# GNN kernel: first stage only counts, sum matrices built later and kept in SBUF, second bias split between PE and VectorE

## The reference, cut to what matters

```python
deg  = segment_sum(ones, dst) + 1 ;  dinv = rsqrt(deg)
conv(x, W, b) = segment_sum((x@W)[src] * dinv[src]*dinv[dst], dst) + dinv**2 * (x@W) + b
x  = l2norm(conv(x0, W1, b1))
f(z) = conv(l2norm(conv(z, Wf1, bf1)), Wf2, bf2) + z
k1 = f(x); k2 = f(x + 0.5*k1); k3 = f(x + 0.5*k2); k4 = f(x + k3)
x  = conv(x + (k1 + 2*k2 + 2*k3 + k4)/6, W2, b2)
```

## Time and profile before

| | |
|---|---|
| median of 3 runs | 9125.33 us (9120.25 to 9130.2) |
| the profiled execution, its time | 9196.13 us |
| span of the profile | 9194.4 us |
| busy: PE, DVE, POOL, ACT | 6718.1, 6441.7, 5499.4, 3381.1 us |
| DMA moved | 1693.27 MB, 184 GB/s over the span |
| first two blocks of `prepare` | until 482.5 us |
| scatter of x | until about 1012 us |
| `local_pass` | about 1042 to 3256 us |
| coupled stages | 3256.9 to about 7560 us |
| attention | to the end |

### The profile page before, as it was taken

The page is one execution under the profiler, slowest core; times in us unless marked ns, Lnnn a source line. Parts: engine busy times, 40 slices in busy tenths (PEclk is TensorE's granted clock), DMA queues, the critical chain, the costliest instruction groups (busy, mean ns, idle before and its releaser), DMA issues. The chain is left out here.

```text
span 9194.4 us, 168134 instructions
## 1 busy us (share of the span) xinstructions
PE 6718.1 (73%) x36044; PEld 5385.6 (59%) x36044; DVE 6441.7 (70%) x17476; ACT 3381.1 (37%) x9316; POOL 5499.4 (60%) x6135
## 2 busy tenths in 40 slices
PE   1600399889988966988897797789666669996665
PEld 0100388888888844766675576667444545554544
DVE  2910388677877888779778977987798981117976
ACT  0000366666666645641361164136100111113323
POOL 0067687777877756755575476557332655545667
PEclk9655799999999977999999999999888985557889
DMA  9333345765444455879879988988898762214544
GB/s 142 86 97 97 100 145 146 123 141 139 143 144 138 139 147 156 249 241 292 250 244 312 315 253 260 335 271 259 280 308 280 210 174 61 60 56 141 169 142 125
DMA packets 1968800, 1693.27 MB, mean 184 GB/s; under 512 B 183280, under 2 KB 1879809, under 8 KB 1968301
## 3 DMA queue, kind: packets, MB, share of 16 engines
q1 hardware_dynamic: 1541549, 1107.88, 42.2%
q0 software_dynamic: 160192, 335.62, 13.1%
q10 hardware_dynamic: 266560, 244.12, 7.8%
HBM read 1063.01 MB, written 624.28 MB: 184 GB/s over the span
## 5 line engine op out<-in xcount | busy, mean ns | idle before, releaser
L1193 PE MATMUL bank<-c_rows,c_sums 128*128 128x256 f32 (+1 forms) x3920 | 1336.0, 425 | 1032.3 <-DVE c_rows L1284 620.7
L680 PE MATMUL bank<-wf_w,c_xt 128*128 128x256 f32 x6272 | 1539.2, 390 | 3.7 <-DVE y L1358 2.6
L1193 PEld LDWEIGHTS bank<-c_rows,c_sums 128*128 128x128 f32 x3920 | 696.7, 203 | 1396.9 <-DVE c_rows L1284 699.3
L1225 ACT ACTIVATE c_xt<-bank 128x512 f32<-128x512 f32 (+1 forms) x980 | 563.5, 575 | 2424.2 <-PE bank L1203 1408.8
L1166 POOL DMA_INDIRECT c_rows<-t_tab,src_row x784 | 872.5, 1113 | 970.7 <-PE bank L1193 807.4
L680 PEld LDWEIGHTS bank<-wf_w,c_xt 128*128 128x128 f32 x6272 | 1231.7, 197 | 185.5 <-issue 3.6
L1284 DVE SCALAR_TENSOR_TENSOR c_rows<-bank,carry,c_rows 32x256 f32<-32x256 f32 (+1 forms) x1950 | 910.6, 467 | 495.6 <-issue 340.5
L1166 POOL DMA_INDIRECT c_rows<-z_tab,src_row x784 | 768.9, 981 | 304.7 <-issue 193.0
L985 DVE TENSOR_TENSOR lx_lo<-bank,lx_hi 128x512 fp32r<-128x512 f32 (+1 forms) x1000 | 658.1, 658 | 350.8 <-ACT lx_hi L930 284.5
L930 ACT ACTIVATE lx_hi<-bank 128x512 fp32r<-128x512 f32 (+1 forms) x1000 | 561.1, 567 | 577.4 <-PE bank L899 457.0
L564 POOL DMA_INDIRECT x_tab<-x_in,stage_pos x396 | 406.3, 1026 | 599.5 <-DMA x_in<-in_x 479.3
(11 more groups left out here) (295 smaller groups left out, 15231.3 us busy)
## 6 DMA issues: line engine op xcount, KB each, us to landing
c_z<-z_tab SPq DMA_DIRECT2D x882, 256.0 KB
c_sums<-sum_tab SPq DMA_DIRECT2D x980, 128.0 KB
z_tab<-lz SPq DMA_DIRECT2D x400, 256.0 KB
t_tab<-lt SPq DMA_DIRECT2D x400, 256.0 KB
z_tab<-y ACTq DMA_DIRECT2D x392, 256.0 KB
c_own<-z_tab SPq DMA_DIRECT2D x392, 256.0 KB
t_tab<-y ACTq DMA_DIRECT2D x392, 256.0 KB
c_own<-t_tab SPq DMA_DIRECT2D x392, 256.0 KB
```

The costliest lines, as they stand in the source:

```text
L680: last = nc.tensor.matmul(out, x(k), w[:, k, :], start=(k == 0), stop=(k == ks - 1))
L1193: nc.tensor.matmul(psum[s % 2][:, i * win:(i + 1) * win], sums[:, s, i, :], rows[:, s, i, 0:win], start=True, stop=True).then_inc(S["summe ...
L1225: nc.scalar.activation(xt[:, s % 2].rearrange("p k n -> p (k n)")[:, 0:n], psum[2 + s % 2][:, 0:n], ACT.Copy).then_inc(S["copied"], 1)
```

## The change

- `prepare`, first block: `floats`, `rows` and `store` are gone from it. `hot_hi` comes from ACT: a Square of (column - upper bits) into a new buffer `away`, then a Relu of (1 - that) into `hot_hi`, 4 and 4 instructions of 396 columns per turn. DVE makes `hot_lo` only; PE waits for both.
- `prepare`, third block: `rows`, `floats` and `store` run here, in the first 49 of the 99 turns, with rings of 4.
- The sum matrices go to one SBUF tensor `sums_all` (100,352 bytes per partition), loaded in the first coupled stage and read by PE in all later ones; the loads of `c_sums` in the other nine stages and of `w_sums` are gone. SBUF for it comes from tensors that now end with `local_pass`.
- PE's part of a coupled stage is unrolled (no loop).
- End stages: the bias of one tile of the pair (r = 1, 2) or of both (r = 3) is a further matmul with 3 contraction rows in `multiply` (`c_degs` times `bf2_rows`); for r = 0 both stay on DVE. `c_degs` is made once (in the mid stage r = 0), stored to `deg_tab`, and loaded per pair by `load_others`.
- For r = 0 and 3 the first instruction of `add_rest` (1327, 1331) moves to ACT as `begin_rest`.
- Four scaled copies of bf2 are no longer made; in `shares_beside_far` several semaphores are merged.

```diff
-def skewed(eng, count, steps, ring=4):
+def skewed(eng, count, steps, ring=4, unrolled=False):
...
-    if turns < 1:
+    if unrolled or turns < 1:
...
+        prepare(nc, a, S, counts, m)
+        local_pass(nc, a, S, counts, m)
+    with nc.sbuf_tensor("sums_all", [P, TE, P], F32) as sums_all:
+        m["sums_all"] = sums_all
+        coupled_stages(nc, a, S, counts, m)
+        attention(nc, a, S, counts, m)
...
-                skewed(sp, turns, [(0, rows), (1, store)], ring=2)
...
+            @block.scalar
+            def _(act):
+                act.wait_ge(S["masks"], 7)
+                act.wait_ge(S["dst_split"], 1)
+
+                def high(j, s):
+                    if not isinstance(j, int) or j >= 1:
+                        act.wait_ge(S["hot_high"], ph.at("hot_high", j - 1))
+                    for i in range(4):
+                        last = nc.scalar.activation(away[:, i, :], cols[:], ACT.Square,
+                                                    bias=minus_hi[:, bass.ds(j * 4 + i, 1)])
+                    last.then_inc(S["away"], 1)
+                    act.wait_ge(S["away"], ph.at("away", j))
+                    for i in range(4):
+                        if not isinstance(j, int) or j >= 1:
+                            act.wait_ge(S["counted"], ph.at("counted", j - 1, i + 1))
+                        nc.scalar.activation(hot_hi[:, i, :], away[:, i, :], ACT.Relu, scale=-1.0, bias=ones[:, 0:1]
+                                             ).then_inc(S["hot_high"], 1)
+                skewed(act, turns, [(0, high), (1, lambda j, s: None)], ring=2)
...
-                        v.tensor_scalar(hot_hi[:, i, :], cols[:], dst_hi[:, t], None, ALU.is_equal)
...
-                skewed(dve, turns, [(0, floats), (0, hots)], ring=2)
+                skewed(dve, turns, [(0, hots), (1, lambda j, s: None)], ring=2)
...
+                        pe.wait_ge(S["hot_high"], ph.at("hot_high", j, i + 1))
...
+                def rows(j, s):
+                    if isinstance(j, int) and j >= builds:
+                        return
+                    if not isinstance(j, int) or j >= 4:
+                        sp.wait_ge(S["row_floats"], pb.at("row_floats", j - 4))
+                    sp.dma_start(rows_i[:, s, :], a["dst_rows"][bass.ds(j * (4 * P), 4 * P)].partition_broadcast(P)
+                                 ).then_inc(S["sums_in%d" % s], 16)
+
+                def store(j, s):
+                    sp.wait_ge(S["sums_built"], pb.at("sums_built", j))
+                    sp.dma_start(m["sum_tab"][bass.ds(j * 4, 4), :, :].rearrange("t p f -> p t f"),
+                                 sums[:, s, :, :]).then_inc(S["stored%d" % s], 16)
+                skewed(sp, builds, [(0, load), (0, rows), (3, store)])
+                for j in range(builds, turns):
+                    load(j, j % 4)
+                for s in range(4):
+                    sp.wait_ge(S["stored%d" % s], pb.ring_end("stored", s))
...
+                def floats(j, s):
+                    dve.wait_ge(S["sums_in%d" % s], pb.ring_at("sums_in", j, s))
+                    if not isinstance(j, int) or j >= 4:
+                        dve.wait_ge(S["stored%d" % s], pb.ring_at("stored", j, s, back=1))
+                    v.tensor_copy(rows_f[:, s, :], rows_i[:, s, :]).then_inc(S["row_floats"], 1)
+                    dve.wait_ge(S["row_floats"], pb.at("row_floats", j))
+                    for i in range(4):
+                        last = v.scalar_tensor_tensor(sums[:, s, i, :], rows_f[:, s, i * P:(i + 1) * P],
+                                                      dst_f[:, bass.ds(j * 4 + i, 1)], (up, down)[i % 2][:],
+                                                      ALU.is_equal, ALU.mult)
+                    last.then_inc(S["sums_built"], 1)
+                skewed(dve, builds, [(0, fill), (2, floats)])
+                for j in range(builds, turns):
+                    fill(j, j % 4)
...
+    if bias:
+        last = nc.tensor.matmul(out, bias[0], bias[1], start=False, stop=True)
...
+    by_pe = [(), (0,), (0,), (0, 1)][r] if end else ()
+    by_dve = [i for i in range(2) if i not in by_pe] if end else []
...
-    n_rest = [1, 1, 1, 4][r] + 1 if end else 1 if final else 0
+    n_rest = [1, 2, 2, 3][r] if end else 1 if final else 0
...
-                    sp.wait_ge(S["summed"], ph.at("summed", j - 4))
-                sp.dma_start(sums[:, s, :, :], m["sum_tab"][bass.ds(j * 2, 2), :, :].rearrange("t p f -> p t f")
-                             ).then_inc(S[f"sums_in{s}"], 16)
-                if past(j, 4):
                     sp.wait_ge(S["u_set"], ph.at("u_set", j - 4))
                 if first:
+                    sp.dma_start(sums[:, bass.ds(j * 2, 2), :],
+                                 m["sum_tab"][bass.ds(j * 2, 2), :, :].rearrange("t p f -> p t f")
+                                 ).then_inc(S[f"sums_in{s}"], 16)
...
+                if by_pe:
+                    sp.dma_start(degs[:, s, :].bitcast(F32), m["deg_tab"][:, bass.ds(j * (2 * P), 2 * P)]
+                                 ).then_inc(S[f"degs_in{s}"], 16)
...
+            if turned_degs:
+                sp.wait_ge(S["degs_split"], 2)
+                for n, part in enumerate((deg_hi, deg_hi, deg_lo)):
+                    for k, tiles_ in enumerate((P, TE - P)):
+                        sp.dma_start(m["deg_tab"][n].rearrange("(t p) -> t p", p=P)[k * P:k * P + tiles_, :],
+                                     part[0:tiles_, k, :].bitcast(F32)).then_inc(S["degs_out"], 16)
+                sp.wait_ge(S["degs_out"], 96)
...
-                    nc.tensor.matmul(psum[s % 2][:, i * win:(i + 1) * win], sums[:, s, i, :], rows[:, s, i, 0:win],
-                                     start=True, stop=True).then_inc(S["summed"], 1)
+                    nc.tensor.matmul(psum[s % 2][:, i * win:(i + 1) * win],
+                                     sums[:, j * 2 + i, :],
+                                     rows[:, s, i, 0:win], start=True, stop=True).then_inc(S["summed"], 1)
...
+                                        (degs[:, s, i * P:(i + 1) * P], m["bf2_rows"][0:3, :]) if i in by_pe else None)
...
-            skewed(pe, pairs, [(0, add_up(0)), (2, turn), (0, add_up(1)), (3, multiply)])
+            if turned_degs:
+                for k, tiles_ in enumerate((P, TE - P)):
+                    last = nc.tensor.transpose(psum[6][0:tiles_, k * P:(k + 1) * P],
+                                               m["c_root_deg"][:, k * P:k * P + tiles_], ident[:])
+                last.then_inc(S["degs_turned"], 1)
+            skewed(pe, pairs, [(0, add_up(0)), (2, turn), (0, add_up(1)), (3, multiply)], unrolled=True)
...
+            def begin_rest(j, s):
+                act.wait_ge(S[f"others_in{s}"], ph.ring_at("others_in", j, s))
+                if past(j, 2):
+                    act.wait_ge(S["taken"], ph.at("taken", j - 2))
+                nc.scalar.activation(rest[:, s % 2, :, :], zs[len(others) - 1][:, s, :, :], ACT.Copy,
+                                     scale=1.5 if r == 0 else -1 / 3).then_inc(S["rest_begun"], 1)
+
             def store(j, s):
                 act.wait_ge(S[done], ph.at(done, j))
                 act.dma_start(tiles(target, j, wout), y[:, s, :, 0:wout]).then_inc(S[f"stored{s}"], 16)
...
             if normed:
                 steps.append((ready, scale))
             steps.append((ready, store))
+            if begun:
+                steps.append((3, begin_rest))
...
-                    rest_step(v.tensor_scalar(pr, zs[0][:, s, :, :], 1.5, None, ALU.mult))
+                    pass
...
-                    rest_step(v.tensor_scalar(pr, zs[3][:, s, :, :], -1 / 3, None, ALU.mult))
+                    dve.wait_ge(S["rest_begun"], ph.at("rest_begun", j))
                     for n, c in enumerate((1 / 3, 2 / 3, 0.5)):
+                        if n:
+                            dve.wait_ge(S["rest_set"], ph.at("rest_set", j, count[0]))
+                        rest_step(v.scalar_tensor_tensor(pr, zs[n][:, s, :, :], c, pr, ALU.mult, ALU.add))
+                if by_dve:
+                    if r == 0:
+                        dve.wait_ge(S["rest_begun"], ph.at("rest_begun", j))
+                    else:
                         dve.wait_ge(S["rest_set"], ph.at("rest_set", j, count[0]))
-                        rest_step(v.scalar_tensor_tensor(pr, zs[n][:, s, :, :], c, pr, ALU.mult, ALU.add))
-                if end:
-                    dve.wait_ge(S["rest_set"], ph.at("rest_set", j, count[0]))
-                    for i in range(2):
-                        last = v.scalar_tensor_tensor(pr[:, i, :], m[f"bf2_{r}"][:], dinv[:, bass.ds(j * 2 + i, 1)],
+                    for i in by_dve:
+                        last = v.scalar_tensor_tensor(pr[:, i, :], scaled_bias[:], dinv[:, bass.ds(j * 2 + i, 1)],
                                                       pr[:, i, :], ALU.mult, ALU.add)
-                    last.then_inc(S["rest_set"], 1)
```

(3 more changed lines are left out.)

203 lines of the change are left out of this document (102 added, 101 removed).

## The result

| | before | changed | ratio |
|---|---|---|---|
| median of 4 runs | 9127.76 us (9120.25 to 9134.89) | 8850.49 us (8848.25 to 8863.71) | 0.9699, 95% interval 0.9683 to 0.9716 |
| profiled execution's span | 9194.4 us | 8850.1 us | |

The change saves 277 us; 263 were forecast.

The account below looks back on a forecast made before the run. Limits were taken stage by stage: DVE, then ACT, in the first block, POOL in the third and mid, DVE in end stages. -221 + 10 - 70 + 54 - 35 - 1 = -263 us from 9125.33 gave 8862 us, range 8790 to 8940.

Parts of the forecast that it names:

- First block, -221: First block: ACT becomes the limit at 4.55 us a turn, so the second block starts at 232 us instead of 453.
- rival B: First block: bound by hand-overs at 5.5 us a turn, not ACT's rate; +46, total 8908 us; chance 15%.
- Third block, +10: Third block: POOL stays the limit; the added casts, comparisons and DMA hide behind it but slow it by 10 us.
- rival C: Third block: POOL loses every DVE instruction in full, 88 us in place of 10; total 8940 us; chance 5%.
- the bound of 0 to 17: Third block: busy DVE and DMA slow POOL's 196 scatters by 17 us at most, 0 at least.
- sign of 530 to 545 us: Third block: the length expected in the changed kernel's profile if the prediction holds, 530 to 545 us.
- End r = 0, +54: End r = 0: DVE waits for begin_rest behind ACT's store, 1.50 us in place of 0.95; pair 4.05 to 4.60 us.
- Rival A: End r = 0 and 3: ACT runs ahead, begin_rest is in time; -49 and -70, total 8724 us; chance 10%.
- End r = 1 and 2, -70: End r = 1 and 2: DVE loses one bias addition worth 0.40 us; pair 4.32 to 3.96 us; bounds -78 and 0.
- Rival E: End r = 1 and 2: DMA holds the pair at 4.3 us, no gain; first block as forecast; total 8932; chance 7%.
- End r = 3, -35: End r = 3: DVE loses work but waits longer after take; pair 6.25 to 5.90 us; bounds +0 and -70.
- Rival D: Coupled stages: PE waits for its written-out code to be fetched; slower, up to 9411 us; chance 3%.

Follow-up runs that it names:

- hot_shared: Changed kernel with one of the four hot_hi of a first-block turn made by DVE in one comparison, ACT making three: 8816.38 us, ratio 0.9651 to before.
- rest_first: Changed kernel with ACT's begin_rest put ahead of the store: 8670.05 us, ratio 0.9486 to before.
- changed_again: Changed kernel, unchanged, measured again on another chip: 8935.41 us, ratio 0.9720 to before.
- before_written_out: Kernel before with only PE's coupled loops written out: 9182.49 us against 9186.4, ratio 0.9993.
- bias_dve: Changed kernel with both bias additions of end r = 1 and 2 back on DVE, sums still in SBUF: ratio 0.9772 to before.
- r0_by_dve: Changed kernel with the first multiplication of c_rest in end r = 0 back on DVE, r = 3 unchanged: 8799.72 us, ratio 0.9632 to before.
- again: Kernel before, unchanged, profiled a second time: 9136.72 us in one execution, span 9135.0 us.

## Why the prediction was right, and where it was off

**First block, -221: right.** 222.8 us less than in the same profile that the forecast was made from. The turn was 4.60 us against 4.55: the instructions are 0.52 apart as forecast, the two waits cost 0.22 each (a lost overlap of 0.09 and 0.12 to 0.14 of gap) instead of 0.2. `hot_shared` shows that ACT's rate was the limit, as said; rival B, bound by hand-overs at 5.5 us a turn, falls. That the clearing "no longer matters" holds for the changed kernel with 50 us to spare (its last DMA lands at 180.2; 189.4 in `rest_first`); in `hot_shared`, with a quarter less on ACT, it was the limit.

**Third block, +10: the sum near, the cost elsewhere.** I had let VectorE slow POOL. It does, by little: in the first profile a scatter of the first half takes 0.970 us on average and one of the second half, beside no building, 0.957, and that is the whole +2.5 us. By the rule of the Trainium skill ("SBUF — State Buffer", § Who interferes with whom) the 49 casts would have kept POOL out for 21 us. The trace agrees with the hold and not with the sum, in which every cast would hold up a scatter for its whole length. Ten held one up, for a part of theirs, as here:

```profile
264.69 0.43 DVE L579 CAST rows_f<-rows_i 128x512 f32<-128x512 int32 x1 [2.38 <-DMA rows_i<-in_dst_rows]
264.74 1.21 POOL L596 DMA_INDIRECT x_tab<-x_in,stage_pos  x1 [0.30 <-issue]
```

A scatter that begins 0.05 us into a cast takes 1.21, one at 0.13 takes 1.12, one at 0.31 its usual 0.96: 1.6 us over these ten. Ten that begin inside a comparison lost 0.6 us together, where the prediction, by the same section, had them lose nothing, and 11 casts that begin inside a scatter were themselves longer, up to 0.64. With this rival C falls. The step that failed is the bound of 0 to 17: it let POOL be slowed by a busy DVE alone and had no term for SP, whose slow instructions cost 43 us of waiting for `x_in` in `changed_again` (+21 for the block against `before_written_out`). The sign of 530 to 545 us was missed as well: it was built on the disturbed profile's scatters of 1.026 us, and the same stretch, from the first scatter to the last, took 502 us.

**Mid, `first`, `last`: 0, right.** Mid stages of 374.4 to 376.4 us against 374.1 to 377.1. In `bias_dve` and `r0_by_dve` the end stages returned to their old lengths though the sums stayed in SBUF, so keeping them there is worth nothing by itself.

**End r = 0, +54: right, step by step.** The chain was 1.54 us in the median against 1.50, the pair 4.64 against 4.60, and the stage longer by 57.6. `rest_first` and `r0_by_dve` show that the chain is all of it. Rival A was the state that `rest_first` brings about: its 8724 became 8670, since r = 3 went beyond what I allowed it.

**End r = 1 and 2, -70: too much.** 24.9 and 22.7 us instead of 35 each. The step that failed is "PE gains one matmul ... on 3.29: not the limit". DVE's work alone would be 3.93 us a pair (3.92 to 3.96 were forecast), but PE's bias product lies on a ring with DVE's `carry_on(1)`, which held the pair at 4.06. The product was also priced too low: one lengthened PE's part of the ring by 0.51 us (2.26 to 2.77), where the forecast had 0.11 to 0.29. An engine with room on average can still be late at a hand-over. Rival E fell: the stages were not held by the DMA engines.

**End r = 3, -35: too little.** 58.8 us. The gap from `take` to line 1418 had a median of 1.39 us instead of 1.50, since the store's issue is the short one there (a median of 0.38); that gives 5.79 by the same sum, and 5.76 was measured, 48 us over the stage. The other 11 us the forecast had at nothing: its pair of 6.25 was one without a wait for PE, and the stage before had 29 such waits, where the changed one has 10 (3.8 us in all), which is most of them:

```profile
DVE c_rows L1284 <- PE bank L1193: 14.5, 29, 1.4
```

The remark that DMA was close behind at 6.0 was wrong, as `rest_first` shows with 4.89 a pair.

**The sum of the coupled stages** was forecast at -51 and came to -53 (against the first profile) or -48 (against `again`): r = 0 off by 4 us, r = 1 and 2 together by 22 and r = 3 by 24 the other way. That the sum is right to 3 us is luck.

**Rival D** falls by `before_written_out`. In the Trainium skill, "Runtime: NRT & Kernel Launch", § Instruction fetch mechanics, says that fetching runs ahead where no branch is taken; by that rule PE's code written out costs nothing, and the run agrees (0.9993).

**The base.** The forecast took the excess of the profiled execution off in full. `again` shows that this was right: its parts lie where the change does nothing. SP's slow instructions are in the first profile (its third block and its local pass) and not in `again`.
